# Four adapter-table products moved behind the first unit's rounded-weight products, with their four copies

## The reference

```
x = x + L0(x)      # quantise/dequantise in 8 groups chosen by |x| against thresholds
x = x + x @ w1[a].T                               # one of 8 full matrices, by the sequence's id a
x = x + x @ W2.T + (x @ lora_A[l]) @ lora_B.T * 0.5     # one common W2, l is a second id
x = x + (x @ B3[a].T) @ A3[a].T                         # rank 16
```

## Time and profile before

| what | value |
| --- | --- |
| median of 3 runs | 486.1 us (485.64 to 488.54) |
| the profiled execution's own time | 486.4 us |
| its span | 484.6 us |
| PE busy | 465.8 us, 96% |
| DVE busy | 418.6 us, 86% |
| ACT busy | 359.5 us, 74% |
| POOL busy | 45.2 us, 9% |
| chain that ended last | PE 83%, DVE 8%, ACT 4%, DMA 2% |
| mean granted TensorE clock | 0.993 of full speed |

### The profile page before, as it was taken

One profiled execution on the slowest core, in us unless ns is written; L12 is line 12 of the kernel. 1 busy time (PEld: TensorE's weight loads), 2 busy tenths in 40 slices (PEclk: granted clock), 3 DMA queues, 4 the chain that ended last, 5 costly groups with the idle time before them and its releaser, 6 DMA issues.

```text
span 484.6 us, 8214 instructions
## 1 busy us (share of the span) xinstructions
PE 465.8 (96%) x3184; PEld 426.1 (88%) x3184; DVE 418.6 (86%) x480; ACT 359.5 (74%) x384; POOL 45.2 (9%) x46
## 2 busy tenths in 40 slices
PE   3999769999999999999999999999999999999997
PEld 3969669899898989899998989899999989899995
DVE  3999999988999899989999899989999899989120
ACT  5989968679787879679787879679787879676011
POOL 1054001200003000200002000200002000100000
PEclk9999979999999999999999999999999999999999
DMA  7997314712236113712326113712336123702002
GB/s 276 402 415 243 131 34 148 292 45 103 90 95 284 43 60 131 276 60 103 106 91 268 44 62 127 287 49 103 118 93 254 43 73 116 289 5 87 1 1 87
DMA packets 17830, 67.07 MB, mean 138 GB/s; under 512 B 2576, under 2 KB 5904, under 8 KB 13712
## 3 DMA queue, kind: packets, MB, share of 16 engines
q1 hardware_dynamic: 17808, 66.81, 37.7%
HBM read 56.84 MB, written 9.96 MB: 138 GB/s over the span
## 4 chain that ended last, share of the span: by engine, by line
PE 83%; DVE 8%; ACT 4%; DMA 2%; issue 1%; POOL 0%; DVEq 0%; SPq 0%; ACTq 0%
PE x_bank L598 45%; PE acc L623 32%; DVE y L460 4%; PE x_bank L611 3%; PE acc L635 2%; PE acc L633 2%; DVE uq L448 1%; ACT tq L329 1%; DMA ua<-w2t 1%; DMA xin<-x 1%; DVE x L473 1%; DVE uq L466 1%; ACT mask L344 1%; DVE tq L439 1%; ACT w2h L400 1%
## 5 line engine op out<-in xcount | busy, mean ns | idle before, releaser
L598 PEld LDWEIGHTS x_bank<-x,w1b 128*128 128x128 f32 x2048 | 234.4, 194 | 8.1 <-issue 4.4
L598 PE MATMUL x_bank<-x,w1b 128*128 128x128 f32 x2048 | 235.8, 277 | 4.0 <-DVE x L473 4.0
L329 ACT ACTIVATE tq<-xin,magic,rdelta 128x1024 f32<-128x1024 f32 x128 | 157.0, 1234 | 3.7 <-DMA xin<-x 3.4
L344 ACT ACTIVATE mask<-absx,negtop 128x1024 bf16<-128x1024 f32 x112 | 128.5, 1147 | 40.8 <-DVE y L460 40.1
L460 DVE COPY_PREDICATED y<-mask,uq 128x1024 f32<-128x1024 int16 x112 | 150.7, 1346 | 0.1
L439 DVE TENSOR_SCALAR tq<-tq,par 128x1024 f32<-128x1024 f32 x128 | 98.5, 769 | 8.5 <-ACT tq L329 4.8
L448 DVE TENSOR_SCALAR uq<-tq,ylow,yhigh 128x1024 f32<-128x1024 f32 x112 | 92.5, 826 | 1.1 <-issue 0.9
L623 PE MATMUL acc<-w2h,x2h 128*128 128x512 f32 x256 | 80.9, 393 | 3.3 <-DVE x2l L479 3.3
L623 PE MATMUL acc<-w2h,x2l 128*128 128x512 f32 x256 | 79.9, 389 | 0.0
L623 PE MATMUL acc<-w2l,x2h 128*128 128x512 f32 x256 | 79.1, 390 | 0.0
L295 POOL TENSOR_TENSOR w1b<-w1b,eye 128x256 f32<-128x256 f32 x32 | 34.6, 1083 | 370.9 <-DMA w1b<-w 370.9
(11 more groups left out here) (56 smaller groups left out, 219.3 us busy)
## 6 DMA issues: line engine op xcount, KB each, us to landing
w1b<-w SPq DMA_DIRECT2D x32, 1024.0 KB, 6.7
xin<-x SPq DMA_DIRECT2D x16, 512.0 KB, 3.7
out<-outb SPq DMA_DIRECT2D x14, 512.0 KB, 2.8
w1b<-w2n SPq DMA_DIRECT2D x4, 1024.0 KB, 10.8
ring<-w2t SPq DMA_DIRECT2D x6, 512.0 KB, 6.3
ua<-e_dram SPq DMA_DIRECT2D x16, 128.0 KB, 2.5
ua<-w2t SPq DMA_DIRECT2D x2, 512.0 KB, 7.2
va<-la SPq DMA_DIRECT2D x8, 128.0 KB, 2.7
```

The source lines that it names most:

```text
L329: nc.scalar.activation(tq[:, n % TQ, :], flat(xin, c % UN), ACT.Identity, bias=magic[:, 0:1], scale=rdelta[:, g:g + 1]).then_inc(t_ready, 1)
L344: nc.scalar.activation(mask[:, n % MK, :], absx[:, :], ACT.Relu, bias=negtop[:, g:g + 1], scale=1.0).then_inc(mask_ready, 1)
L598: last = nc.tensor.matmul(x2_bank[2 * t + i][:, o % HALF * P:(o % HALF + 1) * P], w1b[:, o, at:at + P], x1[:, t, k, :], start=(o % HALF == ...
```

## The change

E's product on PE moves from its place between G and the first W1 product to the place between batch 0's HIGH parts and its LOW parts. Its third and fourth banks are now x2_bank 0 and 1 instead of 2 and 3, which hold unit 0's x2 and are free once x2l of unit 0 is made. PE's own wait for the four copies (`e_ready`) moves from ahead of unit 1's W1 product to behind the second LOW part. ACT's copies move from steps 12, 13, 13, 14 to steps 18, 18, 19, 19.

```diff
-        e_bank = [acc[2], acc[3], x2_bank[2], x2_bank[3]]
+        e_bank = [acc[2], acc[3], x2_bank[0], x2_bank[1]]
...
-        ACT_E = (12, 13, 13, 14)
+        ACT_E = (18, 18, 19, 19)
...
                 if first:
+                    adapters_e()
                     for k in range(HALF):
                         pe.wait_ge(w2l_ready, k + 1)
                         product(0, k, LOW)
-                    pe.wait_ge(e_ready, 2 * EH)
                 pe.wait_ge(x1_ready, UN * b + 2)
                 w1_x1(b, 1, range(OT))
                 if first:
                     for k in range(HALF, KT):
                         pe.wait_ge(w2l_ready, k + 1)
                         product(0, k, LOW)
+                    pe.wait_ge(e_ready, 2 * EH)
...
             bilinear()
             adapters_g()
-            adapters_e()
             batch(0, first=True)
```

## The result

| | median | range | ratio to the kernel before |
| --- | --- | --- | --- |
| before | 486.07 us | 485.64 to 488.54, 4 runs | |
| the change | 492.07 us | 490.24 to 493.26, 4 runs | 1.011, 95% interval 1.0063 to 1.0156 |

The change makes the kernel slower: its median lies 6.0 us higher. The ratio takes in every execution and is not that of the medians; 1.011 is 5.3 us, the distance of the two means. The profiled execution took 491.71 us with a span of 489.9, against 484.6 before.

A forecast was written before the change was run, and what follows sets the result against it. Two paths bound the kernel, PE's and DVE's, with DVE 1.2 us in hand at batch 1. Terms -0.25 + 1.05 + 1.2 + 3.7 gave +5.7, with the clock +8.55: 486.1 + 8.6 = 494.7 us, range 490.2 to 497.3.

The forecast's parts named there:

- PE's own part (-0.25): PE up to unit 1's second LOW part: done at 85.9 instead of 86.15, both waits and the slow clock gone.
- The front: First W1 product, without E ahead: starts at 35.95 at 1.2 GHz, 2.9 to 3.5 slower, ends about 53.4; hidden.
- ACT's stand at the copies: ACT waits for E's last result until 68.1; last copies end at 73.4; DVE loses only its 0.4 lead.
- U: SP's write of E takes until 78.0, then four loads; U is there at 82.3, ACT standing at L370 until 82.4.
- The estimate by the Trainium skill: E's write plus U's loads from fixed costs and bandwidth: 7.3 us instead of 8.9, the end 1.6 earlier.
- DVE 6.8 late: DVE at unit 1's x2l, held behind U in ACT's list: starts at 86.2 instead of 79.42 and stays late.
- The three waits: PE waits for DVE at x2l, at its second half and ahead of batch 1: 1.05, 1.2 and 3.7 us.
- +5.7 predicted: Delay at batch 1's start without a clock fall: -0.25 + 1.05 + 1.2 + 3.7; start at 104.65 instead of 98.96.
- The clock at the new wait (+2.85): TensorE's clock falls at the 3.7 us wait, slowing batch 1's first W1 product: 2.85, bounds 0 and 3.5.
- rival A: The last wait, ahead of batch 1, leaves the clock up: 5.7 alone, 491.8 us; chance 0.33.
- x of unit 3: Its load goes out near 85.4, about ten later; ACT's scaling may wait under 1 us, which ACT has in hand.
- Rival B: Not slower: U lands by about 77 instead of 82.3, E simply fills PE's two waits, 485.8 us; chance 0.06.

The follow-up runs named there:

- a_front_fill: The changed kernel with eight f32 matmuls (6.9 us, results unused) on PE between G and the first W1 product, where E stood: 493.73 us, ratio 1.0173.
- The last step of part 3: The changed kernel with unit 3's x ahead of E's write and U's rounding one step later, then all E copies at step 20: 488.05 before that last edit, 485.99 us with it.
- b_u_late: The kernel before, with batch 0's loads of U held until the fourth tile of unit 1's W1 product, E at its old place: 492.29 us, ratio 1.0133.
- part 1: The changed kernel with batch 0's roundings of U one ACT step later, behind x2h of unit 1, and DVE's split of U at step 24: 492.63 us, ratio 1.0159.
- a_x_first: The changed kernel with SP's load of x for unit 3 issued ahead of E's write, U's rounding unmoved: 492.47 us, ratio 1.0133.
- split_x_u: The changed kernel with E's first two banks back behind G, copies at step 18, unit 3's x ahead of E's write, U at steps 22 and 23: 485.77 us, ratio 1.0002.
- a_fill: The changed kernel with four f32 matmuls (3.4 us, results unused) on PE in the wait ahead of batch 1: 490.81 us, ratio 1.0114.

## Why the prediction was right

- **What held**: slower, by the readers of E and not by PE. The mechanism (copies, write, loads of U, x2h behind U in ACT's list, DVE late, PE waiting ahead of batch 1) is in the trace step by step, and 492.07 lies in the range.
- **PE's own part (-0.25)**: E fills PE's waits, and there is no fall in unit 1's W1 product (14.21 us). The front was misread. The first W1 product started at 34.63, not 35.95, and took 15.66 us: its fall cost 1.45, not 2.9 or more, and it ended at 50.29 instead of 53.4. This is hidden by the wait for x2l, as predicted; a_front_fill shows that. Not foreseen was the slow stretch near 59, which cost 1.6: E started 0.85 after the predicted 61.05, and PE reached unit 1's W2 product 0.7 later than before (86.86 against 86.15) instead of 0.25 earlier. It was not hidden, for E's copies and all that hangs on them came later with it.
- **ACT's stand at the copies**: 8.89 us. I had DVE lose only its lead at step 19; it idled 1.72 + 1.43 there. In the change this is hidden, since DVE had to wait 4.36 at x2h anyway. The last step of part 3 gives a price of about 2 us once U and x are nearly in time, but that edit also brought the write of E forward from 73.08 to 70.47, and no run parts the two.
- **U**: write at 74.3, loads from 78.4, read at 82.28 (predicted 73.4, 78.2, 82.3). The write of E was issued 0.9 late and landed earlier than the 4.2 us taken (median 3.1 from issue to landing). That the two cancel and U's time comes out right to 0.02 us is luck. The estimate by the Trainium skill ("DMA: Bandwidth & Descriptors", "Anatomy of one DMA"), whose figures are for transfers that GpSimd issues and not SP, had 1.6 less for write and loads: 7.3 against 8.9. Measured from 74.30 to 82.28 are 8.0, so the trace lies between the two.
- **DVE 6.8 late**: 6.6 at x2l's first half (86.02 against 79.42), 6.2 at x1 (102.75 against 96.52), since DVE's split of U took 1.22 us here and 1.61 before. The three waits: 1.05 predicted and none of note, 1.2 and 0.49, 3.7 and 3.46. Batch 1 at 104.65 predicted, 104.10 measured; **+5.7 predicted, +5.1 measured**.
- **The clock at the new wait (+2.85)** is the term that was mis-sized: it is 0 in the profiled run, where the 48 matmuls took 5.62 us behind the wait of 3.46. In b_u_late and a_front_fill it was paid in full behind waits of 3.51 and 3.45. What it is in the change's other executions, no trace shows. So rival A is what the profile has, 491.8 against 491.71 (the baselines differ by 0.3). The forecast of 494.7 was 2.6 too high, inside its range. The prediction could not tell from waits of 3.27 and 3.75 on which side 3.7 would fall, and the runs show that waits alike in length went both ways.
- **The cause was half told.** I named U and called x of unit 3 a wait under 1 us, which is what the trace shows (0.94). But part 1 took U out of the way and nothing was won: x, issued at 83.86 there, was late as well and came to light. Rival B's condition, a U that lands by 77, no run tried; such a U would bring forward the x behind it in SP's queue too. A wait that is short because a longer one precedes it isn't small.

## What to carry to other kernels

When work is moved later on the engine that bounds, follow its results through every queue to their last reader, and list what else stands behind them in the same in-order queue: here two loads were late side by side, and each had to be mended before the other's mending showed. Time won for the bounding engine is worth only what the next one has in hand (here DVE, 1.2 us in the kernel before). Price a wait with the clock that may fall behind it. And when the clock differs between two traces, compare distances between instructions before comparing times.

## What the runs showed of the hardware

Whether TensorE's clock falls at a wait is not told by the wait's length here. It stayed at 2.4 GHz through 3.27 us in the kernel before and 3.46 in the change. It fell at 3.44 in a_x_first, 3.45 in a_front_fill and 3.51 in b_u_late, and at 2.87 in split_x_u, ahead of its HIGH part at 56.05. It also fell once PE was already back at work: after 2.34 us of waiting until 56.52, the change's window from 58.09 to 60.65 shows 1.2 GHz. Back-to-back f32 matmuls paid 1.6 to 2.9 us for a fall ahead of batch 1 (7.25 to 8.56 us for 48 that take 5.62). a_fill and a_front_fill, which start batch 1 within 0.04 us of each other, differ by 2.9 us in these 48 matmuls and by 2.9 in the median.

The Trainium skill ("TensorE: Matmul & The Clock Gate", "Why this matters for your kernels") judges a gap between bursts of matmuls by its length. These runs do not bear that out near this length: two waits that are alike within 0.01 us came out differently.
